# An attention and FFN kernel: thirteen tiles of the FFN's quantised hidden rows split in SBUF and turned by DMA instead of TensorE

## What is computed

```python
def fp4_quant_dequant(x):                  # blocks of 16 along the last dim
    scale = max(max(abs(xb)) / 6, 1e-12)   # one per block
    q = GRID[searchsorted(MID, abs(xb / scale))] * sign(xb) * scale
def fp4_linear(x, w):
    return fp4_quant_dequant(x) @ fp4_quant_dequant(w).T

x = x + xattn(layernorm(x), ctx)
x = x + ffn(layernorm(x))
# ffn(x): h = silu(fp4_linear(x, w_gate)) * fp4_linear(x, w_up)     h: 704 wide
#         return fp4_linear(h, w_down)
```

## Time and profile before

| | us |
|---|---|
| median of 3 runs | 409.79 (409.62 to 411.29) |
| profiled execution, its own time | 407.99 |
| its span, first to last instruction | 406.1 |
| PE busy in the span | 334.3 (82%) |
| DVE busy | 307.4 (76%) |
| ACT busy | 264.3 (65%) |
| POOL busy | 252.8 (62%) |
| granted PE clock, mean | 0.975 |

### The profile page before, as it was taken

How to read it: one execution, slowest core, us unless ns; L and a number is a source line. 1 busy time by engine, 2 the same in 40 slices (tenths; PEclk the granted TensorE clock), 3 DMA queues, 4 the chain that set the end, 5 groups by cost and what they waited for, 6 DMA issues and landing times.

```text
span 406.1 us, 9531 instructions
## 1 busy us (share of the span) xinstructions
PE 334.3 (82%) x3595; PEld 255.8 (63%) x3595; DVE 307.4 (76%) x634; ACT 264.3 (65%) x635; POOL 252.8 (62%) x248
## 2 busy tenths in 40 slices
PE   1778678888988979889798685888759999999976
PEld 1455466566776867768676564566537776676764
DVE  1989658446877758677689766388999999999692
ACT  3767969668898998989898876335423454443431
POOL 7362435528787887877977666247663776776510
PEclk9999789999999999999999989699989999999999
DMA  7991537565889978999898788311000000000001
GB/s 212 321 335 34 98 66 123 105 89 96 138 137 174 146 138 138 150 170 139 154 135 170 136 127 145 61 28 28 13 1 15 26 15 16 24 15 25 17 26 40
DMA packets 125375, 40.86 MB, mean 101 GB/s; under 512 B 117452, under 2 KB 123280, under 8 KB 125329
## 3 DMA queue, kind: packets, MB, share of 16 engines
q1 hardware_dynamic: 125329, 40.25, 51.4%
HBM read 8.78 MB, written 2.10 MB: 27 GB/s over the span
## 4 chain that ended last, share of the span: by engine, by line
DVE 43%; PE 30%; issue 11%; ACT 10%; POOL 3%; DMA 2%; SPq 0%; ACTq 0%; DVEq 0%
PE ps L562 5%; DVE arena L1148 5%; PE ps L483 4%; ACT arena L831 4%; PE ps L617 4%; DVE arena L1150 4%; DVE arena L1102 4%; PE ps L485 3%; PE ps L484 3%; DVE negmax L1071 3%; DVE arena L1273 3%; DVE arena L1087 3%; DVE arena L1239 2%; PE ps L578 2%; POOL arena L1344 2%
## 5 line engine op out<-in xcount | busy, mean ns | idle before, releaser
L1344 POOL TENSOR_TENSOR arena<-arena 128x640 f16<-128x640 f32 x64 | 94.7, 1480 | 71.7 <-ACT arena L841 71.6
L831 ACT ACTIVATE arena<-ps,negmax 128x154 f32<-128x154 f32 x256 | 78.7, 401 | 8.4 <-DVE negmax L1071 7.4
L1071 DVE TENSOR_REDUCE negmax<-ps 128x4 f32<-128x616 f32 x64 | 50.9, 796 | 26.3 <-PE ps L617 26.2
L562 PE MATMUL ps<-v_h,pT 128*128 128x132 f16 (+1 forms) x640 | 52.4, 213 | 16.4 <-DVE arena L1087 8.8
L562 PEld LDWEIGHTS ps<-v_h,pT 128*128 128x128 f16 x640 | 38.7, 99 | 22.7 <-issue 21.3
L483 PE MATMUL ps<-arena 128*128 128x256 f16 (+1 forms) x144 | 41.1, 286 | 10.8 <-DVE arena L976 5.8
L1349 POOL TENSOR_TENSOR arena<-arena 128x256 f16<-128x256 f32 x64 | 44.2, 692 | 7.3 <-ACT arena L848 7.3
L841 ACT ACTIVATE arena<-arena 128x640 f16<-128x640 f32 x64 | 47.9, 748 | 1.1
L483 PE MATMUL ps<-arena,xnT_even 128*128 128x352 f16 x128 | 40.7, 318 | 5.3 <-DVE xnT_even L1158 5.3
L484 PE MATMUL ps<-arena 128*128 128x256 f16 (+1 forms) x144 | 41.0, 285 | 0.0
L485 PE MATMUL ps<-arena 128*128 128x256 f16 (+1 forms) x144 | 40.9, 284 | 0.0
(11 more groups left out here) (155 smaller groups left out, 951.5 us busy)
## 6 DMA issues: line engine op xcount, KB each, us to landing
out_dram<-arena SPq DMA_DIRECT2D x16, 128.0 KB, 1.7
pT<-arena SPq DMA_TRANSPOSE x70, 4.1
xs<-in_x_dram SPq DMA_DIRECT2D x2, 512.0 KB, 7.3
arena<-in_L_xattn_w_out_dram SPq DMA_DIRECT2D x1, 1024.0 KB, 11.8
xs<-in_x_dram SPq DMA_DIRECT2D x2, 384.0 KB, 6.6
wffn<-in_L_ffn_w_down_dram SPq DMA_DIRECT2D x1, 704.0 KB, 9.6
wffn<-in_L_ffn_w_gate_dram SPq DMA_DIRECT2D x1, 640.0 KB, 7.9
wffn<-in_L_ffn_w_up_dram SPq DMA_DIRECT2D x1, 640.0 KB, 8.6
```

The costliest lines, as they stand in the source:

```text
L562: last = pe.matmul(o[:, h0 * HB:h1 * HB], pT[:, n % RING_P, part * CHUNKS + c], v[:, b, j, at[0]:at[-1] + 1].rearrange("p m k -> p (m k)") ...
L831: last = act.activation(prob[:, j, k * LP:k * LP + L], ps[:, 2 * (j % 2) + k % 2, (k // 2) * L:(k // 2 + 1) * L], ACT.Exp, bias=negmax[:, ...
L1071: dve.tensor_reduce(negmax[:, s, 4 * j:4 * j + 4].rearrange("p (k u) -> p u k", k=2), v, AX.X, ALU.max, negate=True).then_inc(max_done, 1)
L1344: pool.tensor_tensor(part_of(j, 1), prob[:, j], part_of(j, 0), ALU.subtract).then_inc(p_low, 1)
```

## The change

For tiles 0 to 12 the quantised rows `hq` are no longer turned by PE and split out of PSUM. ACT casts them to fp16 in SBUF (`high_h(t-2)`, L933 of the changed kernel), POOL subtracts the cast from them (`low_h(t-2)`, L1414), both into `hsplit`, which lies where the queries of even steps lay; and one transposing DMA of SP turns high and low part together into `hT`, 12 blocks of 128 by 128 (`turn_h`, L476). `down(t)` waits for that DMA. The factor -HS, which the copies out of PSUM applied, moves into the block scales, so that `hq` holds it. PE, ACT and DVE keep the old way for tiles 13 to 15 only (`high_ht`, `low_ht`), which now have PSUM banks 0, 4 and 2. SP's stores move between the transfers.

```diff
@@ SP
+            def turn_h(t):
+                i, s = step_of(t)
+                sp.wait_ge(h_low, t + 1)
...
+                wait(sp, down_mm, t - 1)
+                sp.dma_start_transpose(hT[:, s].rearrange("p a (c n) -> p (a c) n", n=P),
+                                       hsplit[:, s].rearrange("p a n -> p (a n)")).then_inc(h_turned[s], 16)
...
+            for t in range(2 * STEPS):
+                if t < TURNED_BY_PE: turn_h(t)
+                if t >= DOWN_LAG - 2: store(t - DOWN_LAG + 2)
@@ PE, down
-                pe.wait_ge(ht_low, t + 1)
+                if t < TURNED_BY_PE:
+                    pe.wait_ge(h_turned[s], 16 * (t // 2 + 1))
+                else:
+                    pe.wait_ge(ht_low, t - TURNED_BY_PE + 1)
@@ PE, ffn
                     if exists(summed[0]): down(*summed)
-                    if exists(turned[0]): turn_h(*turned)
@@ ACT
+            def high_h(t):
+                act.wait_ge(hq_done, t + 1)
+                wait(act, h_turned[t % 2], 16 * (t // 2))
...
+                act.activation(hsplit[:, t % 2, 0, 0:F], hq[:, t % 2, 0:F], ACT.Copy).then_inc(h_high, 1)
...
                     if exists(shift(i, s, -1)[0]): magnitude_h(*shift(i, s, -1))
-                    if exists(turned[0]): h_high(*turned)
+                    if 0 <= 2 * i + s - 2 < TURNED_BY_PE: high_h(2 * i + s - 2)
                     if exists(summed[0]): y_copy(*summed)
@@ DVE
-                block_scales(hid[:, s], [blk_h[:, s, r] for r in range(3)], hscaled, t)
+                block_scales(hid[:, s], [blk_h[:, s, r] for r in range(3)], hscaled, t, -HS)
...
-                    if last_tile(i, s): h_low(*shift(i, s, -TURN_LAG))
                     if exists(shift(i, s, -1)[0]): grid_h(*shift(i, s, -1))
                     if last_tile(i, s):
-                        h_low(*shift(i, s, -2))
-                    elif exists(shift(i, s, -TURN_LAG)[0]):
-                        h_low(*shift(i, s, -TURN_LAG))
-                    if last_tile(i, s): quantise_last(i, s)
+                        low_ht(TURNED_BY_PE)
+                        quantise_last(i, s)
@@ POOL
+            def low_h(t):
+                pool.wait_ge(h_high, t + 1)
+                pool.tensor_tensor(hsplit[:, t % 2, 1, 0:F], hq[:, t % 2, 0:F], hsplit[:, t % 2, 0, 0:F], ALU.subtract).then_inc(h_low, 1)
...
-                wait(pool, ht_mm, t - 1)
+                if t >= TURNED_BY_PE + 2: pool.wait_ge(ht_mm, t - 1 - TURNED_BY_PE)
                 pool.wait_ge(hgrid, t + 1)
...
+                    if 0 <= 2 * i + s - 2 < TURNED_BY_PE: low_h(2 * i + s - 2)
                     if exists(shift(i, s, -1)[0]): round_h(*shift(i, s, -1))
```

More of the change, by code:

```diff
@@ L141, in xattn_ffn_kernel @@
         rinv = sb("rinv", [P, 2, 4], F32)
-        below = sb("below", [P, 1], F32)
+        below = sb("below", [P, 2], F32)
         unused = sb("unused", [P, 2], F32)
@@ L200, in xattn_ffn_kernel @@
         hq = take(2 * FP_).rearrange("p (s n) -> p s n", s=2)
-        hT_h, hT_l = (take(FP_).bitcast(F16).rearrange("p (s n) -> p s n", s=2) for _ in range(2))
+        hT = take(2 * FP_).bitcast(F16).rearrange("p (s a n) -> p s a n", s=2, a=2)
+        hsplit = raw["q"][:, 0:2 * FP_].bitcast(F16).rearrange("p (s a n) -> p s a n", s=2, a=2)
         y = take(2 * D).rearrange("p (s n) -> p s n", s=2)
@@ L466, in _, with store @@
                 turn(n)
[L468 to L474, removed]
+            def turn_h(t):
+                i, s = step_of(t)
+                sp.wait_ge(h_low, t + 1)
+                if t == 0:
+                    for j in range(QUADS):
+                        sp.wait_ge(turned[j], 16 * len(range(j, SLOTS + HID_LAG, QUADS)))
+                wait(sp, down_mm, t - 1)
+                sp.dma_start_transpose(hT[:, s].rearrange("p a (c n) -> p (a c) n", n=P),
+                                       hsplit[:, s].rearrange("p a n -> p (a n)")).then_inc(h_turned[s], 16)
+            def store(t):
+                i, s = step_of(t)
+                sp.wait_ge(y_ready, t + 1)
+                sp.dma_start(out[batch(i), rows_of(i, s), :], y[:, s, :]).then_inc(stored[s], 16)
+            for t in range(2 * STEPS):
+                if t < TURNED_BY_PE: turn_h(t)
+                if t >= DOWN_LAG - 2: store(t - DOWN_LAG + 2)
+            for t in range(2 * STEPS - DOWN_LAG + 2, 2 * STEPS):
+                store(t)
             for s in range(B):
@@ L690, in turn_h @@
                     pe.wait_ge(hq_done, t + 1)
[L691 to L693 removed]
+                if t == TURNED_BY_PE:
+                    pe.wait_ge(pad2_zero, 2)
                 else:
@@ L707, in down @@
                 for c in range(FC):
-                    last = three(ps[:, D_BANK, 0:D], hT_h[:, s, c * P:(c + 1) * P], hT_l[:, s, c * P:(c + 1) * P],
+                    last = three(ps[:, D_BANK, 0:D], hT[:, s, 0, c * P:(c + 1) * P], hT[:, s, 1, c * P:(c + 1) * P],
                                  wdT[:, c, 0:D], wdT[:, c, D:2 * D], False, c == FC - 1)
```

77 lines of the change are left out of this document (39 added, 38 removed).

## The result

The changed kernel took 416.59 us (median of 4 runs, 415.49 to 418.49) against 409.71 of the kernel before (407.39 to 411.29): a ratio of 1.016, 95% interval 1.010 to 1.022. It is slower by 6.9 us. The profiled execution took 415.49, with a span of 413.7 (before: 406.1).

A forecast was written before the change was run, and what follows sets the result against it. The prediction took a DVE-POOL-DVE loop, lengthened by the subtraction, as the bound. Start +1.4, ten turns +5.1 and tail -1.55 gave +4.9 us, on a median of 409.79 forecast as 414.7 us, range 411.0 to 418.5.

The forecast's parts named there:

- The bound and its loop: FFN: scales_h(t+1) on DVE waits for POOL's round_h(t-1); the subtraction lengthens this loop, making a pair 15.83 against 15.10 us.
- 13.36 us for DVE's program in a pair: DVE in a middle pair of tiles: without two L1273 splits its own program would need 15.10 - 1.74 us.
- preceded by idle time ended by POOL's L1420 in nearly every tile: Expected profile sign: DVE's L1120 follows such idle time in nearly every tile from 3 to 15.
- 0.14 us of overlap in each collision: POOL and DVE operations on SBUF exclude each other; the later ends its own duration less about 0.14 us behind the release.
- The start: First FFN tiles: low_h(0) ahead of round_h(1) makes scales_h(3) start at 294.04 in place of 292.59, +1.4 us.
- reaches tile 5: Start of the FFN: L1273 left out (-0.87) and grid_x's longer collisions (0.86) cancel, so the +1.4 us stays to tile 5.
- The tail: End of the FFN: the last quantisation begins 2.46 us behind the reciprocal in place of 4.01, -1.55 us.
- what follows is the same: End of the FFN: everything after the last quantisation begins was taken as unchanged.
- priced at nothing: PE's half clock after idle time: a gate_up loses 1.9 us, but PE has 3.1 spare per pair; at most 3 us.
- The idle time of POOL: Rival, chance 0.07: POOL's 4.1 us idle in a pair takes two low_h of 3.0, giving a faster kernel, about 399 us.
- The collisions: Rival, chance 0.10: grid_x's operations do not hold low_h and round_h; an odd turn is 7.6 us, time 411.1.
- The transfers: Rival, chance 0.08: DMA transfers take over 7 us, so down waits; at 8 us the time is 419.7.

The follow-up runs named there:

- e4: Kernel before plus an unused POOL subtraction of the same form at the same place, with no cast or transfer: 418.84 us, ratio 1.019 to the kernel before.
- e1: Changed kernel with POOL's round_h(t-1) put ahead of low_h(t-2): 412.83 us, ratio 1.007 to the kernel before.
- e2b: Changed kernel with four slots in place of two for the hidden rows' block scales, POOL's order kept: 411.85 us, ratio 1.004 to the kernel before.
- e10: Changed kernel with tile 2's subtraction behind the rounding at tile 4, and unused matmuls in PE's two late waits: 415.69 us.
- e7: Changed kernel with only tiles 1, 3, 5, 7, 9, 11 and 12 by DMA and POOL's rounding first: 407.40 us, ratio 0.993 to the kernel before.
- e5: Changed kernel with unused matmuls ahead of PE's transposes of tile 13 and the down projection of tile 12: 416.96 us.
- e11: Changed kernel, odd tiles to 11 and tile 12 by DMA, rounding first, 30 unused matmuls ahead of tile 12's down projection: 408.30 us.
- e12: Changed kernel, only odd tiles to 11 by DMA, rounding first, 25 unused matmuls ahead of PE's transposes of tile 13: 410.24 us.

## Why the prediction came out as it did

The forecast was 414.7 us, with a range of 411.0 to 418.5 and slower by over 0.5% at 0.83. Measured: 416.59, slower by 1.6%.

**The bound and its loop: right.** `scales_h` waits for `round_h`, and the subtraction lengthens that loop by its whole time. Turns of 7.34 and 8.49 were forecast; 7.33 to 7.36 and 8.46 to 8.48 were measured, with one odd turn of 8.24 behind tile 5, where L1122 took 0.19 and not 0.42. The ten turns came to 77.72 (78.0). e4 shows that the subtraction by itself does it, e1 and e2b that the loop does. But the loop is less far ahead of DVE than the prediction has it: its 13.36 us for DVE's program in a pair leaves out the longer hold-ups, with which it is 15.24 (e2b). So the sign "preceded by idle time ended by POOL's L1420 in nearly every tile" came in part: 1.1 to 2.8 us ahead of tiles 3, 7, 11, 14 and 15, some 0.15 ahead of 6, 8, 10, 12 and 13, none ahead of 4, 5 and 9.

**The operations of POOL: right.** L1414 took 1.52 and 1.97 as forecast, L1166 on 512 elements 1.87 (1.9); `scales_h`'s L1122 takes 0.42 in an odd tile (the +0.26 for value_x was 0.23, from 0.19). The reading of the earlier trace rows, 0.14 us of overlap in each collision, held.

**The start: the forecast of 1.4 was too small.** At tile 3 it was right: from `scales_h(2)` to `scales_h(3)` 7.33 in place of 5.88, +1.45. The step that failed is the next one, that L1273 left out and grid_x's longer collisions cancel and the delay then "reaches tile 5". Tile 3 to 4 gave +0.17, and tile 4 to 5 +1.10 (10.69 to 11.79): L1026 +1.28, `scales_x`'s L1122 +0.69 (0.87 in place of 0.18, behind `round_h`), L1273 -0.87. Tile 4 is not like the pair from which the collisions were read, since the layernorm stands in it. The row that could have told was there before the change: L1005 at 1.27 among neighbours of 0.17, held up by `value_h` (L1356, to 305.40).

**The tail: its first part right, "what follows is the same" wrong.** From the end of the reciprocal (395.30) to L1281 are 2.45 us (forecast 2.46). But from L1281 to the end the changed kernel takes 15.95, the kernel before 14.91 (from L1263): +1.04. That is the clock. It was priced at nothing, with up to 3 us at the upper end, since PE has time to spare in a pair; this holds in the pair (15.81 with a mean clock of 0.89, 15.82 with 1.00) but not in the tail, where DVE's last splits wait for PE. With full clock (e10) the tail is 18.89, 1.59 below that of the kernel before: the forecast's 1.55. Two figures of the prediction's clock do not come out of its own rows, without effect on the forecast: a gate_up of 3.6 us would lose about as much again at half speed and not 1.9 (the 18 matmuls of a `down` took 3.84 us at 0.50 and 1.96 at 1.00), and 414.7 and 3 us are 417.7 and not 417.5.

So the sum is +0.55 ahead of tile 2, not part of the change, +1.45 at tile 3, +1.27 in the two tiles behind it, +4.83 and -0.50: 7.6. With the two omitted terms taken out by e10 it reads +1.43, +5.19 and -1.59, together +5.0 against the forecast's +4.9.

**The rivals.** The idle time of POOL could not take the work: e2b has the loop open, and still a pair of 15.24. That rival gave DVE the whole 1.74 that it is spared; the hold-ups beside the subtractions take 1.88 of it back (14.93 busy in place of 14.79). On POOL, 11.01 busy and two subtractions of 1.52 and 1.97 are 14.5, which in 15.10 leaves 0.6, about the one wait of e2b. The collisions came in the forecast's order in all odd turns. The transfers landed in time in the middle (3.7 in the median, below the 4.1 of the earlier trace rows); they appear as waits only in the tail. The Trainium skill's "might not help" (Perfetto Trace Analysis, Optimizing Scalar/DVE Operations), of work that goes from one of DVE and POOL to the other, is mild for all thirteen tiles: the move costs 7.0 us from tile 2 on (126.4 against 119.4). For half of the tiles, with the rounding first, it gains 1.7 (e7).

## What to carry to other kernels

Idle time of an engine inside a loop of two engines is not room: put the added operation into the loop and count one turn, collisions included, and then add up what both engines would be busy if the loop were opened, with the time that each holds up the other, since the second sum can be above the old pace as well. Apply a collision rule that was read in one stretch to every stretch where the new operation will stand, down to operations on a few elements. And where other work hides an engine at half clock, say up to where: the last tiles have no such cover.

## What the runs showed of the hardware that was not expected

A DVE operation on 128x6 int32 elements lasted 1.45 us in place of 0.17 beside a subtraction of POOL. PE's clock fell to 0.50 during the second of two waits of 2.13 and 1.47 us close to each other, was back at 1.00 some 6.6 us later, and stayed at 1.00 when 28 matmuls of no use stood in these waits (e5, e10). A transposing transfer of 12 blocks landed after 3.7 us in the median, and in one place after 4.1 us (e7) or 5.5 us (e11, e12) in different runs. With its loop open (e2b), DVE was busy 14.93 us of a pair though two of its operations had gone, since others were held up by POOL's for 1.88 us more.
